# Decay attention of a vision tower: tokens in time order, queries against a prefix of keys, one exponent product, scores in alternating row halves

## What is computed

```python
xn = (x - mu) / sqrt(var + 1e-5) * gamma + beta
q, k, v = heads(xn @ Wq), heads(xn @ Wk), heads(xn @ Wv)      # 8 heads of 64
alpha = sigmoid(heads(xn @ Wa + ba))
k = k / max(norm(k), 1e-12)
def step(S, inp):                                             # over the 37 tokens
    q_t, k_t, v_t, a_t = inp
    S = a_t[..., None] * S + k_t[..., None] * v_t[..., None, :]
    return S, einsum('bhji,bhj->bhi', S, q_t)
_, outs = scan(step, 0, (q, k, v, alpha))
out = outs @ Wo + x
```

## Time and profile before

| | |
|---|---|
| median of 3 runs | 1512.55 us (1509.75 to 1514.78) |
| the profiled execution | 1507.89 us, its span 1505.9 us |
| TensorE matmul, busy | 1217.7 us (81%) |
| TensorE weight loads, busy | 987.3 us (66%) |
| VectorE / ScalarE / GpSimd, busy | 817.7 / 582.0 / 408.8 us |
| score matmuls of this stage (line 1490) | 704 instructions, 80.4 us busy, 280 ns mean |
| their weight loads | 704 instructions, 79.1 us busy |

### The profile page before, as it was taken

The page is one execution under the profiler, slowest core; times in us unless marked ns, Lnnn a source line. Parts: engine busy times, 40 slices in busy tenths (PEclk is TensorE's granted clock), DMA queues, the critical chain, the costliest instruction groups (busy, mean ns, idle before and its releaser), DMA issues. The chain is left out here.

```text
span 1505.9 us, 25717 instructions
## 1 busy us (share of the span) xinstructions
PE 1217.7 (81%) x9477; PEld 987.3 (66%) x9477; DVE 817.7 (54%) x1652; ACT 582.0 (39%) x1111; POOL 408.8 (27%) x450
## 2 busy tenths in 40 slices
PE   5898445999999737879798999999995888888463
PEld 5786134888888415668678999999982555555332
DVE  4456464354453289845534444343362677776675
ACT  2353633444443376335352333332221343343460
POOL 0123234233230154322321111111103435434103
PEclk9998676787787668889989999999995899999785
DMA  5100201000000000020011100130001000000001
GB/s 161 61 3 2 90 12 48 1 1 0 0 0 1 33 1 0 1 86 2 3 42 43 43 20 23 42 127 0 0 1 62 1 1 1 0 0 1 1 0 33
DMA packets 11341, 35.66 MB, mean 24 GB/s; under 512 B 3026, under 2 KB 6017, under 8 KB 9584
## 3 DMA queue, kind: packets, MB, share of 16 engines
q1 hardware_dynamic: 11248, 34.42, 6.5%
HBM read 33.20 MB, written 1.21 MB: 23 GB/s over the span
## 5 line engine op out<-in xcount | busy, mean ns | idle before, releaser
L143 PE MATMUL psum<-L2f_XT_high,L2f_EW_high 128*128 128x444 f32 (+1 forms) x384 | 136.7, 356 | 9.0 <-issue 5.1
L2183 DVE TENSOR_TENSOR L2f_prod<-psum,L2f_act 128x444 f32<-128x444 f32 (+1 forms) x96 | 55.8, 582 | 148.2 <-ACT L2f_act L2104 148.2
L2104 ACT ACTIVATE L2f_act<-psum 128x444 f32<-128x444 f32 (+1 forms) x96 | 48.9, 511 | 222.7 <-PE psum L143 222.7
L143 PE MATMUL psum<-L2f_XT_high,L2f_EW_low 128*128 128x444 f32 (+1 forms) x384 | 134.9, 351 | 0.0
L143 PE MATMUL psum<-L2f_XT_low,L2f_EW_high 128*128 128x444 f32 (+1 forms) x384 | 134.3, 350 | 0.0
L2069 POOL TENSOR_TENSOR L2f_EW_low<-weights_even,L2f_EW_high 128x1024 fp32r<-128x1024 f32 x24 | 58.1, 2426 | 265.4 <-ACT L2f_EW_high L2083 265.4
L143 PE MATMUL psum<-L2f_EW_high,L2f_H_high 128*111 128x256 f32 x352 | 99.4, 282 | 2.6 <-issue 2.6
L143 PE MATMUL psum<-L2f_EW_low,L2f_H_high 128*111 128x256 f32 x352 | 98.8, 281 | 0.0
L143 PE MATMUL psum<-L2f_EW_high,L2f_H_low 128*111 128x256 f32 x352 | 98.4, 280 | 0.0
L662 PE MATMUL psum<-weights_odd,L_cT 128*111 128x512 f32 x132 | 70.3, 658 | 22.5 <-DVE L_rot L505 17.5
L143 PEld LDWEIGHTS psum<-L2f_XT_high,L2f_EW_high 128*128 128x128 f32 x384 | 73.5, 191 | 15.5 <-issue 8.5
(11 more groups left out here) (367 smaller groups left out, 3063.0 us busy)
## 6 DMA issues: line engine op xcount, KB each, us to landing
weights_even<-experts SPq DMA_DIRECT2D x8, 1536.0 KB, 6.5
weights_even<-L_w SPq DMA_DIRECT2D x4, 1024.0 KB
patch_ring<-patches SPq DMA_DIRECT2D x11, 333.0 KB, 4.0
weights_odd<-L_wqkv SPq DMA_DIRECT2D x2, 768.0 KB
out<-X SPq DMA_DIRECT2D x10, 111.0 KB
weights_odd<-L_wo SPq DMA_DIRECT2D x1, 1024.0 KB
weights_even<-tok_w SPq DMA_DIRECT2D x1, 768.0 KB
weights_even<-L_wg SPq DMA_DIRECT2D x1, 768.0 KB, 4.7
```

The costliest lines, as they stand in the source:

```text
L143: mm = core.nc.tensor.matmul(out, left[a], right[b], start=first and n == 0, stop=last and n == len(passes) - 1)
L2104: nc.scalar.activation(act_[:, p, 0:k * R], core.bank(p)[:, 0:k * R], ACT.Silu).then_inc(act_done, 1)
L2183: nc.vector.tensor_tensor(prod[:, c, 0:w_], core.bank(2 + c % 2)[:, 0:w_], act_[:, c % 2, 0:w_], ALU.mult).then_inc(prod_done, 1)
```

## The change

`decay_attention` is rewritten in these respects.

- Rows of a tile inside the stage are ordered by token first and image second. The transposes of the input write their columns in that order (a step of three elements in PSUM), and the values product writes its output back in image order (again a step of three).
- A block of ten tokens is then 30 adjacent queries, and the keys that it may meet are the first 30, 60, 90 or 111 rows. Scaled keys are kept for these prefixes only (`KEYS`), 291 columns in place of 444, and the score matmul has 30, 60, 90 or 111 stationary columns.
- The constants for the query factor and for the key factors stand in one matrix of 111 + 291 = 402 columns. One product per feature group (two passes) gives both, and one exponential follows. Before it were eight passes of 112 columns and eight of 444, and five exponentials.
- The score matmuls go block by block, and within a block the row half alternates from one matmul to the next. Both halves end together, and their two masked copies follow one wait.
- Scaled keys are computed block by block over all four feature groups (four operations of 120, 240, 360 and 444 elements a partition).
- The order of the projections is a, k, q, v in place of q, k, v, a; so is the order in which the weights are split at the start. The transposes of k come ahead of those of q. The output projection writes bank 4, and the banks of the projections change with it. The log decay of tile f is made in the middle of the body.

The diff, cut to its core (removed lines that the listing above shows are left out in part):

```diff
+KEYS = [0]
+for _b in range(NBLK):
+    KEYS.append(KEYS[-1] + PER * min((_b + 1) * BLOCK, T))
+DECAYS = R + KEYS[-1]
...
-        dec_q, dec_k = sb("decay_q1", [128, RE], F32R), sb("decay_k1", [128, NBLK * R], F32R)
+        decay = sb("decay_sums", [128, DECAYS], F32R)
...
-        EQ = sb("EQ", [128, 4, R])
-        EK = sb("EK", [128, 2, NBLK * R])
+        E = sb("E", [128, 4, DECAYS])
         kT = sb("kT", [128, 4, R])
         QS = sb("QS", [128, 4, R])
-        KS = sb("KS", [128, 4, NBLK, R])
...
-                for n, c in enumerate("qkva"):
+                for n, c in enumerate("akqv"):
...
+                    def exps(c):
+                        act.wait_ge(e_ps, 4 * g + (c + 1))
+                        if c == 0:
                             after(act, qs_done, g)
+                            after(act, ks_done, NBLK * g)
+                        nc.scalar.activation(E[:, c], core.bank(2 + c % 2)[:, 0:DECAYS], ACT.Exp).then_inc(e_done, 1)
+                    if G:
+                        exps(0)
+                        exps(1)
+                    if O:
+                        act.wait_ge(oT_ps, t + 1)
+                        after(act, y_ps, t - 1)
+                        nc.scalar.activation(OT[:, pt], cols(core.bank(4)[:, 0:4 * R], 4, R), ACT.Copy).then_inc(oT_done, 1)
+                    if F:
                         act.wait_ge(xT_ps, f + 1)
                         after(act, a_ps, f - 1)
                         nc.scalar.activation(xT[0][:, pf], cols(core.bank(5)[:, 0:KD * R], KD, R), ACT.Copy).then_inc(xT_high, 1)
+                    if G:
+                        exps(2)
+                        exps(3)
                         act.wait_ge(kT_ps, g + 1)
+                        after(act, ks_done, NBLK * g)
                         nc.scalar.activation(kT[:], cols(core.bank(5)[:, 0:4 * R], 4, R), ACT.Copy).then_inc(kT_done, 1)
+                    if F:
                         act.wait_ge(k_ps, f + 1)
                         after(act, kT_ps, f - 1)
                         after(act, n2_ready, f - 1)
                         nc.scalar.activation(k[:R, pf], core.bank(7)[:R, :], ACT.Copy).then_inc(k_done, 1)
                         act.wait_ge(a_clamped, f + 1)
                         nc.scalar.activation(la[:R, pf], la[:R, pf], ACT.Exp, scale=-1.0)
                         act.drain()
                         nc.scalar.activation(la[:R, pf], la[:R, pf], ACT.Ln, bias=1.0)
                         act.drain()
+                        after(act, e_ps, 4 * (f - 1))
                         nc.scalar.activation(laT[0][:R, pf], la[:R, pf], ACT.Copy).then_inc(la_high, 1)
+                        act.wait_ge(q_ps, f + 1)
+                        after(act, qT_ps, f - 1)
+                        nc.scalar.activation(q[:R, pf], core.bank(6)[:R, :], ACT.Copy).then_inc(q_done, 1)
...
+                    if F:
+                        dve.wait_ge(a_ps, f + 1)
+                        after(dve, la_low, f - 1)
+                        nc.vector.tensor_tensor(la[:R, pf], core.bank(6)[:R, :], w["L1_ba"], ALU.add)
+                        dve.drain()
+                        nc.vector.tensor_scalar(la[:R, pf], la[:R, pf], LOGIT_FLOOR, None, ALU.max).then_inc(a_clamped, 1)
+                    if G:
+                        dve.wait_ge(e_done, 4 * (g + 1))
+                        dve.wait_ge(kT_done, g + 1)
+                        after(dve, s_ps, g)
+                        for b in range(NBLK):
+                            lo, hi = KEYS[b], KEYS[b + 1]
+                            nc.vector.tensor_tensor(KS[:, :, lo:hi], E[:, :, R + lo:R + hi], kT[:, :, 0:hi - lo], ALU.mult).then_inc(ks_done, 1)
+                        dve.wait_ge(qT_ps, g + 1)
+                        nc.vector.tensor_tensor(QS[:], cols(core.bank(5)[:, 0:4 * R], 4, R), E[:, :, 0:R], ALU.mult).then_inc(qs_done, 1)
+                    if F:
...
-                    if live(i, 3):
+                    if O:
                         dve.wait_ge(y_ps, t + 1)
-                        nc.vector.scalar_tensor_tensor(z[:R, pt], X[:R, t, :], 2.0, core.bank(7)[:R, 0:D],
+                        nc.vector.scalar_tensor_tensor(z[:R, pt], X[:R, t, :], 2.0, core.bank(4)[:R, 0:D],
                                                        ALU.mult, ALU.add).then_inc(z_done, 1)
...
+                    if F:
+                        dve.wait_ge(la_high, f + 1)
+                        nc.vector.tensor_tensor(laT[1][:R, pf], la[:R, pf], laT[0][:R, pf], ALU.subtract).then_inc(la_low, 1)
+                    if O:
                         dve.drain()
                         nc.vector.bn_stats(stat[:R, pt], z[:R, pt])
                         dve.drain()
                         nc.vector.bn_aggr(mv[:R, pt], stat[:R, pt]).then_inc(var_ready, 1)
...
+                    if F:
+                        dve.wait_ge(rn_ready, f + 1)
+                        dve.wait_ge(v_ps, f + 1)
+                        after(dve, oT_ps, f - 1)
+                        nc.vector.tensor_tensor(cols(V[:R, pf], nh, hd), cols(core.bank(7)[:R, :], nh, hd),
+                                                n2[:R, pf].unsqueeze(2).broadcast_to([R, nh, hd]), ALU.mult).then_inc(v_done, 1)
+                    if G:
+                        dve.wait_ge(s_ps, g + 1)
+                        after(dve, oT_ps, g)
+                        dve.sem_inc(mask_turn, 1)
                         scores_out(0)
                         scores_out(1)
...
+                    F, G, O = live(i, 1), live(i, 2), live(i, 3)
+                    def exponents(c):
+                        if c == 0:
                             pe.wait_ge(la_low, g + 1)
+                        after(pe, e_done, 4 * g + (c - 1))
+                        split_matmul(core, core.bank(2 + c % 2)[:, 0:DECAYS], [x[:R, pg, c * 128:(c + 1) * 128] for x in laT],
+                                     [decay[:R]], True, True).then_inc(e_ps, 1)
+                    def transposes(src):
+                        for c in range(4):
+                            mm = nc.tensor.transpose(core.bank(5)[:, c * R:(c + 1) * R], src[:R, pg, c * 128:(c + 1) * 128], core.ident[:R, :R])
+                        return mm
+                    if G:
+                        exponents(0)
+                        exponents(1)
+                    if O:
+                        pe.wait_ge(v_done, t + 1)
+                        pe.wait_ge(s_done, 2 * (t + 1))
+                        after(pe, z_done, t)
+                        for h in range(nh):
+                            po = h % 2 * hd
+                            mm = nc.tensor.matmul(core.bank(4)[po:po + hd, h // 2 * R:(h // 2 + 1) * R].rearrange("p (i t) -> p t i", i=PER),
+                                                  V[:R, pt, h * hd:(h + 1) * hd],
+                                                  PM[:R, h % 2, (h // 2) * R:(h // 2 + 1) * R], start=True, stop=True)
+                        mm.then_inc(oT_ps, 1)
                     if F:
                         pe.wait_ge(x_staged, f + 1)
+                        after(pe, qs_done, f - 1)
+                        for c in range(KD):
+                            mm = nc.tensor.transpose(core.bank(5)[:, c * R:(c + 1) * R].rearrange("p (t i) -> p i t", i=PER),
+                                                     xin[:R, pf, c * 128:(c + 1) * 128], core.ident[:R, :R])
+                        mm.then_inc(xT_ps, 1)
                     if G:
+                        exponents(2)
+                        exponents(3)
                         pe.wait_ge(xT_low, upto(i))
+                        pe.wait_ge(k_done, g + 1)
+                        transposes(k).then_inc(kT_ps, 1)
                     if F:
                         pe.wait_ge(xT_low, f + 1)
+                        after(pe, q_done, f)
+                        project(core.bank(6), pf, 0).then_inc(a_ps, 1)
+                    if G:
+                        pe.wait_ge(kT_done, g + 1)
+                        pe.wait_ge(q_done, g + 1)
+                        transposes(q).then_inc(qT_ps, 1)
+                    if F:
                         after(pe, v_done, f)
+                        project(core.bank(7), pf, 1).then_inc(k_ps, 1)
+                        pe.wait_ge(a_clamped, f + 1)
+                        project(core.bank(6), pf, 2).then_inc(q_ps, 1)
+                    if O:
+                        pe.wait_ge(oT_done, t + 1)
+                        for c in range(4):
+                            mm = nc.tensor.matmul(core.bank(4)[:R, 0:D], OT[:, pt, c, :], wo[:, c, :], start=c == 0, stop=c == 3)
+                        mm.then_inc(y_ps, 1)
+                    if F:
+                        pe.wait_ge(k_done, f + 1)
+                        project(core.bank(7), pf, 3).then_inc(v_ps, 1)
                     if G:
+                        pe.wait_ge(ks_done, NBLK * (g + 1))
                         pe.wait_ge(qs_done, g + 1)
```

(25 more changed lines are left out.)

164 lines of the change are left out of this document (10 added, 154 removed).

## The result

The changed kernel takes 1418.42 us, the median of four runs (1413.10 to 1431.45), against 1511.15 (1504.36 to 1514.78, four runs) for the kernel before: a ratio of 0.940, 95% interval 0.933 to 0.948. The forecast was 1420.6 and the range 1405 to 1444. The profiled execution takes 1413.1 us, its span 1411.3, against a forecast of 1415.9 for that execution.

The account below looks back on a forecast made before the run. TensorE's queue was taken to bound the decay stage: a tile falls from 22.8 to 14.9 us, saving 85 us between first and last score, plus 6 and 1 at the ends: 1512.55 - 92 = 1420.6 us, range 1405 to 1444.

Parts of the forecast that it names:

- The sum: One tile of TensorE's queue rebuilt at full clock: 13.7 us of work plus 1.2 of new waits, 14.9 us.
- wait before the values (a): TensorE idles 0.65 us before the values product, as both score copies now come after the last score.
- wait before the transposes of k (b): TensorE idles 0.5 us until bank 5 is read: values end, copy of OT, xT_high, xT_low.
- Two halves load side by side: Score matmuls alternating row halves overlap their weight loads: 0.098 us a pair of 111 columns; burst 2.6 us a tile.
- the straight line for the widths: Score pair distance falls linearly with stationary columns: 0.030, 0.055, 0.080, 0.098 us taken for 30, 60, 90, 111.
- The ends: Outside the stage's first-to-last-score span (85 us less), the start saves 6 us (3 to 8), the end 1 (0 to 4).
- The clock: TensorE's granted clock stays at 1.0 in the stage's steady state; each us at 0.5 costs 0.4.
- the clock still falls in part: Rival: 3.4 to 6.8 us of each tile at half clock, 15 to 31 us more, 1436 to 1452; chance 0.14.
- The halves don't overlap: Rival: score row halves load one by one, 1.7 us more a tile, 1440; chance 0.11, shared with dear narrow loads.
- Narrow loads stay dear: Rival: narrow score loads cost as much as 111 columns, 11 us more; chance 0.11, shared with halves not overlapping.
- Stepped writes to PSUM: Step-three writes by values and input transposes cost nothing; doubled, 11 us, 1432; rival with longer chains, chance 0.10.
- Changes of shape: Each change of score width costs about 0.1 us on TensorE, three a tile, already in the 2.6 us for scores.

Follow-up runs that it names:

- the kernel with the waits filled: Changed kernel with input transposes and the last two exponent groups issued ahead of the values product, ScalarE's OT copy after the exponentials; 1404.16 us, ratio 0.926.
- the two executions profiled later: The changed kernel, unaltered, run and profiled again as yardstick in experiment groups 1 and 2; medians 1410.12 and 1415.81 us.
- the kernel with the halves in turn: Changed kernel with the row half as outermost score loop, all of one half and then the other; 1472.68 us, ratio 0.972.
- the one step above: Kernel before with alternating scores, plus a's projection issued ahead of v's; 1475.38 us, ratio 0.973, against 1482.99 us, ratio 0.979, with alternating scores alone.

## Why the prediction came out

*What bounds the stage* is confirmed. TensorE is busy for 13.77 us of a tile of 14.55, and the rest is its two new waits; VectorE has 9.37 us of work in 14.55 and ScalarE 8.50, against the 10.5 and 9 that the prediction had. No other engine became the bound.

*The sum.* The rebuilt tile, term by term, from the starts in the fence above:

| term | predicted | measured |
|---|---|---|
| scores | 2.6 | 2.45 |
| exponents | 1.7 | 1.67 |
| projections and output projection | 7.3 | 7.55 |
| transposes of k, q and the input | 1.1 | 0.87 |
| values | 1.0 | 0.91 |
| wait before the values (a) | 0.65 | 0.66 |
| wait before the transposes of k (b) | 0.5 | 0.44 |
| tile | 14.9 | 14.55 |

The waits are counted from start to start here (the brackets, 0.50 and 0.29, leave out the ends of the passes before them). What the projections take more is mostly the entry after another kind of product, which the prediction did not count for them: the three that follow one last 1.47, 1.46 and 1.68 us to the next step, the one that follows a projection 1.41, where 1.37 was taken for each; the output projection itself takes 1.53 of the 1.8. All other work is a little shorter. That the median came out within 2.2 us of the forecast is partly luck, since the four executions alone lie 18 us apart; the difference of the two medians is 92.7 us, the sum said 92.

*Two halves load side by side*: right, and with it the straight line for the widths. Pairs start 97, 80, 55 and 30 ns apart against 98, 80, 55 and 30. (The prediction gave the line's values for 60 and 90 columns as 0.050 and 0.075; through its two points they are 0.055 and 0.080, which is what it took in the end.) Of the three changes of width only two cost anything: from 111 to 90 columns none, from 90 to 60 and from 60 to 30 some 0.11 us each (one distance longer by 0.09, the next by 0.02).

*The ends.* The start brings 262.88 - 255.67 = 7.2 us (predicted 6; the first number is in the earlier trace rows), 0.7 of it ahead of the stage's first product, which starts at 232.82 and started at 233.54, where nothing was changed. Exponents begin at 245.75, predicted 246. The end of the stage, behind the last score, takes 12.8 us instead of 13.5: 0.7 (predicted 1). Between the first and the last score 86.6 (85). Together 94.5, predicted 92.

*The clock* was assumed at 1.0 and is 0.98. One tile in ten has 6.8 us at half clock (3.4 in one of the three profiled executions). It takes 16.83 us instead of 14.55, so a us at half clock costs 2.28 / 6.8 = 0.34, where the prediction had 0.4. The two waits shrink in it; in the kernel with the waits filled, where there are none to shrink, a tile with 3.4 us at half clock takes 15.24 us, and (15.24 - 13.78) / 3.4 = 0.43. Which tile it is differs: it was the first of the ten in the two executions profiled later and the sixth in this one. In each of them the fall came within 2 us behind the end of a burst. The rival "the clock still falls in part" was this, in one tile of ten instead of in each: 2.3 us, where it was priced at 15 to 31. The four executions stand in the order of their mean clock as well: 1413.1 us at 0.900, 1414.1 at 0.898, 1422.8 at 0.892, 1431.5 at 0.881. Whether the slower ones lose it in this stage is not shown, since in each group the fastest was profiled, and the stages behind scatter too.

One reading of the clock in the kernel before was short. The prediction has it at half for 6.8 us of a tile "as now", because its row ends there; the stretch goes on (columns as in the earlier trace rows):

```profile
335.10:345.30 10.20, 10.20 (x56) 9.43 (x56) 2.94 (x7) 3.30 (x5) 0.19 (x1) 0.50 0.00 0
```

So it is in seven of the ten tiles, and 6.8 us in three. Priced as the prediction does, a changed kernel that kept this would have been 10.2 x 0.4 x 11 = 45 us slower instead of 31. It also means that much of the gain is the clock's: the ten tiles before hold 222.83 x 0.21 x 2 = 94 us at half clock, those of the changed kernel 6.8, and at 0.4 each, an estimate, that is 35 of the 80.5 us between them. The prediction had this inside its sum, since it set a tile rebuilt at the full clock against one of 22.8 us as measured, but did not name it as a share of the gain.

*The rivals' prices were wrong where their place was right.* "The halves don't overlap" was priced at 1.7 us a tile and 1440; the kernel with the halves in turn takes 1472.7. "Narrow loads stay dear" was a bound of 11 us; it is 23 to 29. The queue's part is close both times: 2.2 a tile less the 0.5 of a wait that it covers, so 1.7, where the prediction had left out the covered wait and some of the loads' cost and hit the 1.7 by luck; and 0.76 a tile, where 1.0 was taken. The failed step is that the prediction kept the clock at 1.0 in these cases, though it had said itself that each fall follows scores: the clock measured in them is 0.78 and 0.81. Had one of them come true, the time would have been outside the range or at its upper end.

*Stepped writes to PSUM*: nothing, as taken. Sixteen value instructions with a step of three last 0.99 us, (0.99 - 0.26) / 15 = 0.049 apart, the distance of the gapless ones in the earlier trace rows. At the half clock the same sixteen take 1.75 us with the step (332.42, changed kernel) and 1.75 without it (line 1508). The Trainium skill, PSUM — Partial Sum Buffer, Specifications (TRN2), says that any non-contiguous access slows matmuls significantly; this measurement, with four-byte elements at a step of three, speaks against it.

*Changes of shape*: the Trainium skill, TensorEngine Tiling (Array Packing), Key Properties, says that switching the tiling mode drains the engine. The trace fits this, with 0.11 us for a switch from 90 to 60 and from 60 to 30 columns and none from 111 to 90, which the list of modes there (128, 64 and 32 columns) would put in one mode. That the cost is a drain the trace does not show.

*What the sum did not say* is which edit earned the gain. I had listed eight passes at 1.86 us as removed; in the changed kernel putting the like of them back costs a tile nothing. The alternation brings 34 us on the kernel before and 55 in the stage at the end of the list. The order by token and the single product of the exponents were not tried by themselves, and the earlier log decay only as the one step above. The parts don't add up, since each works through the same two things: which wait is covered, and whether the burst is short enough for the clock to stay.

## To carry to other kernels

Rebuild the queue of the bounding engine start by start and put the new waits in: that gives the total to a few per cent, while the price of a single removed step says little, since a wait may take its place and a shorter stretch may uncover a chain that it hid. Where the clock falls behind a certain kind of work, price each variant twice, with the clock held and with the clock falling in each tile; here the second price was about three times the first. Independent work issued ahead of a product that waits is worth its wait, some 7 us here for a reordering of a few lines.

## What the hardware showed that I had not expected

- The clock falls with TensorE hardly idle: in the kernel with the halves in turn it is busy for 190.70 of 192.08 us and the clock is 0.78 over them. In the changed kernel it idles for 7.8 of 142.3 us, and the clock is 0.98. What differs between the two is the order of the scores alone, a burst of 4.6 us at the full clock (6.1 as it ran) against 2.5.
- The same 64 instructions in two pieces with 512-column passes between them keep the clock at 0.96 where in one piece it was 0.81, in the profiled executions; over all executions of the two kernels the mean clock is 0.890 to 0.900 against 0.874 to 0.886.
- The time of a load of 64 rows goes with its columns down to 30 (97, 80, 55 and 30 ns for 111, 90, 60 and 30), and a change from 111 to 90 columns costs nothing, while 90 to 60 and 60 to 30 cost about 0.11 us each.
- Writes to PSUM with a step of three elements are as fast as gapless ones: 0.049 us between instructions.
